# The ten one-hot places of expert 0 are written by GpSimd instead of VectorE

## The reference

```
h   = tokens(x)                                  # 1184 x 256
h   = h + attention(layernorm(h))
xf  = layernorm(h)
gates = softmax(xf @ w_router + b_router);  topv, topi = top_k(gates, 2)
pos = running count of the tokens that chose the same expert
buf[e, pos] = xf[token]          if pos < 185    # the expert's rows
out = gelu(buf @ w1 + b1) @ w2 + b2              # per expert
y   = sum over a token's two experts of gate * out[e, pos]  /  sum of its kept gates
h   = h + y
```

## Time and profile before

| what | value |
|---|---|
| time, median of 3 runs | 159.5 us (159.48 to 162.51) |
| span of the profiled execution | 157.9 us; its whole time is not recorded beside the span |
| busy | PE 148.0 us (94%), PEld 138.4 (88%), DVE 105.5 (67%), ACT 82.8 (52%), POOL 50.9 (32%) |
| chain that ended last, by engine | PE 65%, DMA 11%, DVE 7%, ACT 6%, issue 3%, POOL 3% |
| granted clock of PE, mean over the span | 0.989 of full speed |

### The profile page before, as it was taken

One profiled execution on the slowest core, in us unless ns is written; L12 is line 12 of the kernel. 1 busy time (PEld: TensorE's weight loads), 2 busy tenths in 40 slices (PEclk: granted clock), 3 DMA queues, 4 the chain that ended last, 5 costly groups with the idle time before them and its releaser, 6 DMA issues.

```text
span 157.9 us, 2961 instructions
## 1 busy us (share of the span) xinstructions
PE 148.0 (94%) x982; PEld 138.4 (88%) x982; DVE 105.5 (67%) x330; ACT 82.8 (52%) x210; POOL 50.9 (32%) x55
## 2 busy tenths in 40 slices
PE   7999999999999979999999999999999999999950
PEld 6548999899789768899799899999999999999940
DVE  0074994769887898981396859669486694785710
ACT  3222754644317998857066557474682665737100
POOL 6001200505530000005437167084371661604361
PEclk9999999999999999999999999999999999999995
DMA  5999960079000345301499897888868978600422
GB/s 169 406 420 435 394 230 0 0 243 338 5 0 22 138 163 184 116 0 28 97 349 292 272 269 194 269 192 307 269 130 270 262 250 264 131 7 0 48 25 23
DMA packets 16978, 28.46 MB, mean 180 GB/s; under 512 B 1133, under 2 KB 13591, under 8 KB 16585
## 3 DMA queue, kind: packets, MB, share of 16 engines
q1 hardware_dynamic: 14505, 25.49, 46.6%
q0 software_dynamic: 2464, 2.86, 10.6%
HBM read 24.21 MB, written 4.14 MB: 180 GB/s over the span
## 4 chain that ended last, share of the span: by engine, by line
PE 65%; DMA 11%; DVE 7%; ACT 6%; issue 3%; POOL 3%; SPq 1%; POOLq 1%; DVEq 0%
PE ps L1298 20%; PE ps L1333 10%; PE ps L1132 6%; PE ps L1223 6%; DMA w_even<-w 5%; DMA first_t<-first 4%; PE ps L1335 4%; PE ps L1240 3%; ACT xn L556 2%; PE ps L1165 2%; PE ps L1343 2%; PE ps L1310 2%; DMA rows_in<-xrows,src_row 2%; PE ps L1261 2%; ACT xn L565 2%
## 5 line engine op out<-in xcount | busy, mean ns | idle before, releaser
L497 POOL DMA_INDIRECT out_rows<-out_s,dst_row x16 | 23.8, 1485 | 38.4 <-ACT out_s L682 32.1
L658 ACT ACTIVATE first_t<-ps,b_cur 128x186 f32<-128x186 f32 x64 | 23.0, 413 | 23.5 <-PE ps L1298 22.0
L1333 PE MATMUL ps<-hid_hl,split 128*128 128x372 f32 x96 | 29.1, 369 | 0.0
L1335 PE MATMUL ps<-hid_hl,split 128*128 128x186 f32 x96 | 23.9, 249 | 0.0
L1298 PE MATMUL ps<-first_t,patch_t 128*128 128x186 f32 x128 | 21.7, 322 | 0.1
L977 DVE CAST hid_hl<-first_t 128x372 fp32r<-128x372 f32 x28 | 10.7, 383 | 15.9 <-ACT first_t L658 15.9
L1298 PEld LDWEIGHTS ps<-first_t,patch_t 128*128 128x128 f32 x128 | 20.1, 190 | 0.4 <-issue 0.4
L482 POOL DMA_INDIRECT rows_in<-xrows,src_row x14 | 15.6, 1113 | 11.0 <-DVE src_row L945 7.1
L1298 PE MATMUL ps<-first_t,w_even 128*128 128x186 f32 x112 | 18.9, 321 | 0.0
L522 ACT ACTIVATE split<-patch_t 128x512 fp32r<-128x512 f32 (+2 forms) x28 | 14.4, 577 | 8.1 <-DMA patch_t<-patches 5.7
L1335 PEld LDWEIGHTS ps<-hid_hl,split 128*128 128x128 f32 x96 | 18.3, 191 | 0.0
(11 more groups left out here) (179 smaller groups left out, 263.2 us busy)
## 6 DMA issues: line engine op xcount, KB each, us to landing
w_even<-w SPq DMA_DIRECT2D x8, 1024.0 KB, 5.7
patch_t<-w SPq DMA_DIRECT2D x8, 1024.0 KB, 5.5
att<-attn SPq DMA_DIRECT2D x1, 1280.0 KB, 9.4
patch_t<-patches SPq DMA_DIRECT2D x1, 1188.0 KB, 14.0
patch_t<-patches SPq DMA_DIRECT2D x1, 1080.0 KB, 11.5
first_t<-first SPq DMA_DIRECT2D x1, 978.0 KB, 7.0
out_rows<-h SPq DMA_DIRECT2D x2, 384.0 KB, 2.5
xrows<-xn SPq DMA_DIRECT2D x2, 384.0 KB, 3.5
```

Of the source, the lines that this page charges most:

```text
L497: pool.indirect_dma_start(out=out[:, :], out_offset=bass.IndirectOffsetOnAxis(ap=dst_row[0:SIZES[s], c:c + 1], axis=0), in_=out_s[q][0:SIZ ...
L658: ins = act.activation(hid[:, f, :], bank(pair)[:, (f % 2) * SL:(f % 2 + 1) * SL], ACT.Gelu, bias=b1_cur[q][:, f:f + 1])
L1333: pe.matmul(dst[:, 0:2 * SL], w2_h[q][:, f, cols], hid_hl[:, f].rearrange("p a s -> p (a s)"), start=f == 0, stop=False)
L1335: ins = pe.matmul(dst[:, 0:SL], w2_l[q][:, f, cols], hid_hl[:, f, 0], start=False, stop=f == KF - 1)
```

## The change

DVE still computes the column `place0`, and now signals it by a new semaphore. The ten comparisons that write `onehot` stand in POOL's program, behind its products and ahead of its wait for the stored rows. PE waits for `onehot` as before, tile by tile.

```diff
-        slots_known = sem("slots_known")
+        slots_known, place0_ready = sem("slots_known"), sem("place0_ready")
...
                 pool.wait_ge(scaled, POOL_ORDER.index(n) + 1)
+
+            for n, (t0, c) in enumerate(CHOICES):
+                pool.wait_ge(place0_ready, n + 1)
+                for i in range(t0, t0 + c):
+                    pool.tensor_scalar(onehot[:, i], iota_slot[:, 1:SL + 1], place0[:, i:i + 1], None, ALU.is_equal
+                                       ).then_inc(onehot_ready, 1)
...
                 filled(dve, "slots", g)
-                step(dve.scalar_tensor_tensor(place0[:, ts], slots_of(g)[:, :, 0], 1.0, chosen[:, ts, 0], ALU.add, ALU.mult))
-                for t in range(t0, t0 + n):
-                    dve.tensor_scalar(onehot[:, t], iota_slot[:, 1:SL + 1], place0[:, t:t + 1], None, ALU.is_equal
-                                      ).then_inc(onehot_ready, 1)
+                dve.scalar_tensor_tensor(place0[:, ts], slots_of(g)[:, :, 0], 1.0, chosen[:, ts, 0], ALU.add, ALU.mult
+                                         ).then_inc(place0_ready, 1)
```

## The result

The changed kernel took **162.4 us** (median of four runs, 161.2 to 165.1) beside 159.5 us of the kernel before on the same chip (159.1 to 162.5): a ratio of 1.015 [1.008, 1.022]. Forecast were 159.6 us and a range of 159.2 to 161.0. The change is slower by 0.8 to 2.2%, so "within 2%" holds for its middle, and the time lies outside the range. Run again in a later comparison, the same kernel gave 161.7 us, with a ratio of 1.011 [1.007, 1.016] (experiment 5). Ratios here leave out the runs that lay over 1.5% above the fastest of their kernel, and the medians keep them, which is why 162.4 / 159.5 is a little more than 1.015.

What follows compares the result with a forecast made beforehand. The prediction took expert 0's start on PE to be set through ACT's exponential, which DVE awaits, so freeing DVE gains nothing: 159.5 + 0 gained + 0.13 lost + 0 for the pick = 159.6 us, range 159.2 to 161.0.

Steps and rivals of the forecast that it cites:

- the price of POOL's comparison: Length d of one 128 x 186 comparison on POOL: taken as 0.40 us, bounds 0.22 and 0.57.
- 62.54 + 4d: Second half: when POOL's fourth comparison, of length d, reaches PE; 64.14 at d = 0.40, pick 0.25 us late, cost 0.
- the cover of 0.48: PE's wait for DVE's copy before expert 0, hiding a late second pick by 0.48 us; gone at d = 0.46.
- a lock at `logit`: First half: POOL's sixth comparison holds the shared SBUF ports, delaying DVE's first `logit` and what follows by 0.13 us.
- Later tiles are no limit: First pick: a tile keeps PE busy 0.63 us against POOL's 0.36, so POOL's later comparisons don't delay PE.
- theory B: Follow-up theory: the first half pays for the loss, because POOL holds DVE up; no chance given.
- The gain is 0: Removing ten comparisons from DVE gains 0 at the end, since DVE already waits for ACT in both halves.
- L1310 is still let go by DVE's copy: Expected sign in the changed profile: PE's start of expert 0 is still released by DVE's copy.
- let go by the pick itself: Sign of being wrong: PE's start of expert 0, L1310, is released by the second pick.
- the first rival: POOL compares at the two-input rate, d about 0.5 to 0.57, costing at lock and pick: 160.0 to 160.9 us; chance 0.22.
- The third rival: POOL's comparison far slower, working through; expert 0 starts at 59.02 + 10d, over 2% slower from d = 1.0; chance 0.05.
- theory C: Follow-up theory: PE's pauses cost it its clock, making runs slower; no chance given.

Runs made afterwards that it cites:

- experiment 5: The changed kernel run again, unaltered, in a later comparison: 161.7 us, ratio 1.011 [1.007, 1.016] to the kernel before.
- experiment 1: The kernel before plus eight POOL operations at the start (comparisons, addition and product with a column, comparison with a constant, copy, sum of two tensors): 159.0 us, single run.
- experiment 3: The changed kernel with only the second half's four comparisons on POOL, the first half's six staying on DVE: 160.6 us, ratio 1.006 [1.001, 1.010].
- experiment 7: The kernel before with DVE's copy moved ahead of its wait for the exponential and ACT's ahead of the Gelu table load: 159.2 us, ratio 0.995 [0.992, 0.998].
- experiment 10: The kernel before without its four late comparisons, tiles 6 to 9 of the one-hot matrix left empty: 159.3 us, ratio 0.9995 [0.997, 1.002].
- experiment 4: The changed kernel with PE's second pick going tile by tile instead of half by half: 162.2 us, ratio 1.010 [1.001, 1.020].
- experiment 6: The changed kernel with five unread products on PE ahead of the first pick, filling its pause: 162.1 us, ratio 1.013 [1.008, 1.018].
- experiment 11: The changed kernel with POOL comparing only 94 of the 186 slots, the upper 92 left out: 160.3 us, ratio 1.005 [1.002, 1.008].
- experiment 2: The changed kernel with only the first half's six comparisons on POOL, the second half's four staying on DVE: 160.3 us, ratio 1.005 [1.000, 1.009].
- experiment 12: The changed kernel with the second pick tile by tile and five unread PE products ahead of the first pick: 161.2 us, ratio 1.011 [1.006, 1.017].

## Why the prediction was wrong

**The step that failed** is the price of POOL's comparison, "Bounds: 0.22 and 0.57 ... so I take d = 0.40, near the copy". It measured 0.74, outside both bounds. The two rows beneath them were fair: a copy of 186 columns took 0.33 us (0.35 worked out), a sum of two tensors 0.49 (0.57 worked out). What failed is the assumption that the operation lies between them because it streams one tensor as the copy does. By experiment 1 an operation of a tensor and a column is dearer than either. The Trainium skill, page "GPSIMD Engine Reference", section "4.1 Engine selection", calls one-input elementwise work there roughly line-rate; here that holds for the copy at most. The 12 cycles an element that the Trainium skill gives for data-dependent branching in section "3.1 Elementwise — side-by-side cycle accounting" of that page, an estimate of 1.86 us here, didn't come about either: 0.74 us, and an addition takes as long.

**The second half** went as the prediction's own formula says once d is put in. It has the comparison reach PE at 62.54 + 4d; with 0.74 that is 65.50, 1.61 later than tile 9's records stood before, and less the cover of 0.48 it costs 1.13. Measured are 1.46. From its rows the changed kernel's half adds up as 0.26 (`place` to POOL's start) + 3.21 (four comparisons) + 0.05 (POOL's end at 66.21 to PE) + 1.69 (ten records, 66.26 to 67.95) = 5.21. Against the formula the four comparisons are 0.37 longer, mostly the tenth, which took 1.04 beside DVE's `marks` (65.10 to 65.59); the hand-overs are 0.15 shorter than the 0.31 and 0.15 taken; the ten records take 1.69 instead of 1.58. 1.13 + 0.37 - 0.15 + 0.11 = 1.46. In experiment 3, where `marks` began 0.36 us behind the fourth comparison (64.58 and 64.22) and not ahead of it, that one took 0.74, the four 2.95 us, and the half costs less, 1.29. The break point of d = 0.46 follows from the cover, which experiment 7 confirmed.

**The first half** was called +0.13, by a lock at `logit`. That place was wrong. The first `logit` began at 59.65, some 0.3 us into POOL's third comparison, and two of them took 0.36 (0.37 in the earlier trace rows), `nmr` 0.15. The +0.39 has another cause, again the length. PE starts the first pick 58.75 - 57.51 = 1.24 behind `place`, before 58.11 - 57.36 = 0.75: +0.49. "Later tiles are no limit" failed as well. The rows of before that this rests on are

```profile
61.37 0.30 PE L1271 MATMUL ps<-chosen,ones 128*128 128x32 bf16 x6
61.37 0.23 DVE L795 TENSOR_TENSOR is_one<-cst,which 128x64 f32<-128x64 f32 x1
```

POOL's 0.73 a tile is more than PE's 0.63, and from the pick's start to the first count after it there are 62.28 - 58.75 = 3.53 us instead of 3.26 (61.37 - 58.11): +0.27. The next count, L1277, which needs `chosen`, then follows after 0.16 instead of 0.51 (61.88 - 61.37), the last 0.21 of which had been a wait for DVE: -0.35. 0.49 + 0.27 - 0.35 = 0.41, with 0.02 back at `place`. `chosen` came late too (`is_one` took 0.46 us, 0.23 in the kernel before), but it was there at 62.19 and PE took L1277 up at 62.44. So DVE being held up, theory B's reason, did not set this half's length.

**What held.** The gain is 0 (experiment 10), and L1014 begins 0.03 us after ACT's exponential, which ended at 64.62. Its idle time is 0.40, not 1: the second `place` comes 0.54 us later than before (62.74 and 62.20) and the exponential only 0.12 (64.33 and 64.21), and DVE's operations from `upper` on take 0.20 us longer beside POOL. Of the signs that I named, "about 0.36 apart", a longer first `logit` and "L1310 is still let go by DVE's copy" were refuted, and the sign of being wrong, "let go by the pick itself", came. "PE waits on POOL's `onehot` in the second pick" was right.

**The rivals.** What happened is the first rival's mechanism at a larger size: it gave 160.0 to 160.9 up to d = 0.57. Its part by the lock didn't come. Its rate of 2.3 ns a column is close to the 2.5 of experiment 1, and what it lacked is the fixed part, 0.28 instead of 0.15; but its reason, a second operand, doesn't hold, for with a constant the operation still takes 0.67. The third rival's formula, 59.02 + 10d, gives 66.42 at 0.74, too early by 1.4 when the first `place`, 0.15 later here, is counted in. 0.78 of it is POOL's wait for the second `place`: it does not work through.

**The rest of the time.** Expert 0 to the end of the span takes 159.4 - 67.95 = 91.45 us here and 91.95 before. The change need not be the cause: in experiment 10, where expert 0 starts at 65.95 as before, it is 157.5 - 65.95 = 91.55, and over all profiled runs the weight load of expert 2 alone varies between 7.0 and 7.7 us. The 1.85 us at expert 0 and the 1.8 of the repeat's medians agree. The first 162.4 us hold more, and this goes with the clock: of those four runs only the profiled one (161.2 us) had a mean granted clock of 0.989, the others 0.972 to 0.984 (162.0 to 165.1 us). In the repeat the four runs at 0.989 or more took 160.9 to 161.5 us, mean 161.3, beside a mean of 159.5 for the 15 runs of the kernel before at 0.991 to 0.995. So the change costs about 1.8 us, or 1.1%, at such a clock, and theory C may have a share in the 1.015. Where in the runs without a profile the clock fell is not recorded.

## What to carry to other kernels

An operation that the trace does not show on an engine is not bounded by its neighbours in form: a tensor with a column of scalars cost more on POOL than a copy and more than two tensors. Where a step hangs on one unknown price, put the price into the formula and ask what it does at twice the value: the formula for the second half was right to 0.33 us, and its input was not. Work that stands in the chain of waits is worth its length only if the next instruction was not already waiting for somebody else, and the start 0.03 us after another engine's end shows that it was.

## What the runs showed of the hardware

- POOL's operation of a tensor with a column: 0.74 us for 186 columns of f32, 1.20 for 372, the same for `is_equal`, `add` and `mult`; 0.67 with a constant; copy 0.33; two tensors 0.49. Beside DVE's `marks`, which began 0.07 us ahead of it, one comparison took 1.04.
- DVE beside POOL's comparison: `is_one`, two tensors in, began 0.03 us after a comparison's start and took 0.46 instead of 0.23, as if let go about 0.26 us into 0.74. `slot_q` (begun 0.12 us in, 0.32 instead of 0.18) and `got` of experiment 3 (begun 0.13 us in, 0.30 instead of 0.17) give the same 0.26. `upper`, one tensor in, ended at 63.78, with POOL's seventh (63.00 + 0.74), and took 0.36 instead of 0.18. `logit`, begun 0.3 us into a comparison, was not held at all. The Trainium skill, page "SBUF — State Buffer", section "Who interferes with whom", has the loser blocked for the whole instruction, where a VectorE instruction has two SBUF inputs or is in a 2-port mode, which `tensor_scalar` can enter. The row of `upper`, a `tensor_scalar`, fits that, those of `is_one`, `slot_q` and `logit` don't. In the earlier trace rows `nmr` had been held to the end of a POOL subtraction of two tensors; why the comparison lets go earlier is open.
- The granted clock fell to 0.50 within the picks in the profiles of experiments 4, 6 and 11, after pauses of PE of 0.2 to 1.4 us, and in that of experiment 5 at 58.1 us, within PE's pause of 1.36 us ahead of the first pick. All four have POOL's comparisons. It stayed at 1.00 from 57 to 71 us in the changed kernel's own profile and in those of experiments 2, 3 and 12, with pauses of 0.2 to 1.4 us too. What decides between them is open. A low mean clock is not the change's alone: it was 0.985 or less in 7 of the changed kernel's 12 runs and in 7 of the 23 of the kernel before beside the repeat.
